# A DLRM tower: tables of 128 rows, ten features looked up by matmul, a ring of row buffers and a new order of steps

## What is computed

```python
e = jnp.stack([tbl_0[ids[:, 0]], ..., tbl_26[ids[:, 26]]], axis=1)      # (512, 27, 128)
z = jnp.einsum('bnd,bmd->bnm', e, e)[:, i, j]                           # i, j = triu_indices(27, k=1): 351 pairs
h = jnp.concatenate([z, dense_ctx], axis=1)                             # (512, 367)
h = jnp.maximum(h @ W_top1 + b_top1, 0.0)                               # 512 wide
h = jnp.maximum(h @ W_top2 + b_top2, 0.0)                               # 256 wide
y = h @ W_top3                                                          # (512, 1)
```

## Time and profile before

| | us |
|---|---|
| median of 3 runs | 169.3 |
| lowest, highest | 168.25, 169.31 |
| profiled execution: span, first to last instruction | 166.6 |
| around the span, by the median | 2.7 |
| PE busy | 119.2 (72%) |
| DVE, ACT busy | 66.6, 65.0 |
| POOL busy (the 72 gathers are 77.2 of it) | 78.1 |

### The profile page before, as it was taken

One profiled execution on the slowest core, in us unless ns is written; L12 is line 12 of the kernel. 1 busy time (PEld: TensorE's weight loads), 2 busy tenths in 40 slices (PEclk: granted clock), 3 DMA queues, 4 the chain that ended last, 5 costly groups with the idle time before them and its releaser, 6 DMA issues.

```text
span 166.6 us, 1949 instructions
## 1 busy us (share of the span) xinstructions
PE 119.2 (72%) x712; PEld 103.3 (62%) x712; DVE 66.6 (40%) x135; ACT 65.0 (39%) x107; POOL 78.1 (47%) x80
## 2 busy tenths in 40 slices
PE   6439949376357095870798997442399999999995
PEld 6437728255245083650677996441299999799993
DVE  3537539372520553770304650200071464346221
ACT  3050948555490553621904650210062263245110
POOL 2377777777777687887800077777200000000000
PEclk9975999999978969699579999655558999999999
DMA  2344444444445466994300036122115003300600
GB/s 47 117 165 145 158 156 159 160 157 156 155 160 162 152 125 161 208 204 148 95 16 4 0 112 142 47 63 51 31 45 115 0 4 102 57 0 29 134 0 4
DMA packets 15751, 16.45 MB, mean 99 GB/s; under 512 B 10099, under 2 KB 12211, under 8 KB 15614
## 3 DMA queue, kind: packets, MB, share of 16 engines
q1 hardware_dynamic: 13308, 11.35, 22.6%
q0 software_dynamic: 2304, 4.72, 11.6%
q10 hardware_dynamic: 130, 0.26, 0.6%
HBM read 14.62 MB, written 1.71 MB: 98 GB/s over the span
## 4 chain that ended last, share of the span: by engine, by line
PE 51%; issue 19%; DMA 12%; another core or an unknown queue 7%; ACT 5%; DVE 4%; SPq 1%; DVEq 0%; ACTq 0%
PE psG L319 18%; PE psG L302 12%; DMA table<-in_tbl 12%; PE psH L333 8%; PE psH L363 5%; PE psT L282 4%; DVE hot L416 3%; PE psG L345 2%; ACT ET L483 1%; PE psH L376 1%; ACT parts L495 1%; ACT hot L502 1%; ACT hot L506 1%; DVE parts L421 1%
## 5 line engine op out<-in xcount | busy, mean ns | idle before, releaser
L269 POOL DMA_INDIRECT rows<-in_tbl,ids_sb x72 | 77.2, 1072 | 38.8 <-issue 21.0
L302 PE MATMUL psG<-hot,parts 125*128 125x512 f32 x156 | 47.7, 470 | 31.3 <-issue 13.9
L302 PEld LDWEIGHTS psG<-hot,parts 125*128 125x128 f32 x156 | 35.8, 235 | 42.1 <-issue 28.5
L319 PE MATMUL psG<-ET 128*122 128x104 f32 x256 | 31.7, 279 | 7.6 <-issue 6.8
L319 PEld LDWEIGHTS psG<-ET 128*122 128x122 f32 x256 | 30.1, 194 | 8.4 <-issue 8.3
L416 DVE TENSOR_SCALAR hot<-pick_ids,row_no 125x512 fp32r<-125x512 int32 x65 | 26.7, 482 | 19.8 <-remote 11.3
L431 DVE COPY gram<-psG 26x208 f32<-26x208 f32 (+1 forms) x17 | 8.2, 485 | 31.9 <-remote 14.5
L523 ACT COPY gram<-psG 26x208 f32<-26x208 f32 (+1 forms) x17 | 8.3, 489 | 31.2 <-PE psG L319 14.3
L421 DVE TENSOR_TENSOR parts<-table,parts 125x1024 fp32r<-125x1024 f32 (+1 forms) x9 | 11.8, 1313 | 20.8 <-ACT parts L495 18.2
L483 ACT COPY ET<-psG 128x512 f32<-128x512 f32 x9 | 9.8, 1085 | 19.1 <-remote 10.4
L495 ACT CAST parts<-table 125x1024 fp32r<-125x1024 f32 (+1 forms) x8 | 9.0, 1128 | 17.5 <-DMA table<-in_tbl 17.5
(11 more groups left out here) (27 smaller groups left out, 45.3 us busy)
## 6 DMA issues: line engine op xcount, KB each, us to landing
table<-in_tbl SPq DMA_DIRECT2D x6, 500.0 KB
pick_ids<-in_picked_ids SPq DMA_DIRECT2D x8, 250.0 KB
table<-in_tbl SPq DMA_DIRECT2D x3, 625.0 KB
pair_blocks<-gram SPq DMA_DIRECT2D x8, 176.0 KB, 1.9
rows<-in_tbl,ids_sb POOLq DMA_INDIRECT x72
w_sb<-in_w SPq DMA_DIRECT2D x1, 1024.0 KB
zT<-pair_blocks SPq DMA_DIRECT2D x12, 60.5 KB
w_sb<-in_w SPq DMA_DIRECT2D x1, 512.0 KB
```

Of the source, the lines that this page charges most:

```text
L269: pool.indirect_dma_start(out=rows[:, t % 2, f, :], out_offset=None, in_=gathered_tables[f], in_offset=bass.IndirectOffsetOnAxis(ap=ids_sb ...
L302: last = pe.matmul(psP[:, k % 2, :], parts[:, k % 2, x, c, :], hot[:, k % 2, c, :], start=x == 0 and c == 0, stop=x == 1 and c == CH[k] - 1)
L319: last = pe.matmul(o, stationary, group[:, :, 1:F], start=True, stop=True)
```

## The change

- V, the partitions of a looked-up table, goes from 125 to 128. The host pads the ten tables with zero rows to 1024 or 1280; a partition still has 8 or 10 rows.
- PICKED goes from 9 to 10: one table of 1250 rows more is looked up, 17 features are gathered (68 indirect DMAs), and a tile's last quad has one feature. BY_ACT changes with it: two chunks only for every other pick with 10 chunks.
- `table` and `pick_ids` have three buffers (TABLES), so SP's waits refer to pick k-3.
- `rows` becomes a ring of 8 quads (RING) over all tiles: the gathers of quad n wait for the transposes of quad n-8.
- The host lays the ids of the gathered features out as one run per partition, and the load (L213) is one plain copy.
- In the loop of the picks the transposes lag by one (LAG), and nine quads, not five, are transposed there.
- `steps` is written anew.

```diff
-    V = 125
+    V = P
-    BY_ACT = [1 if k < NQ else 2 for k in range(FP)]
+    BY_ACT = [1 if CH[k] == min(CH) or k % 2 else 2 for k in range(FP)]
+    TABLES = 3
+    RING = 8
+    LAG = 1
+    DURING_PICKS = FP - LAG
...
-        rows = sb("rows", [P, 2, FG, D])
+        rows = sb("rows", [P, RING, 4, D])
...
-        BY_DVE = [n >= NQ and n % 2 == (NQ + (n // NQ == T - 1)) % 2 for n in range(T * NQ)]
+        BY_DVE = [n >= DURING_PICKS and n % 2 == 0 for n in range(T * NQ)]
...
+        steps = interleaved(units(0), quads(DURING_PICKS, 2 * NQ)) + quads(2 * NQ, 2 * NQ + 2)
+        steps += interleaved(units(1), quads(2 * NQ + 2, 3 * NQ))
+        steps += mlp(0) + quads(3 * NQ, 3 * NQ + 1) + units(2) + [("layer3", 0)]
+        steps += quads(3 * NQ + 1, 3 * NQ + 2) + mlp(1) + quads(3 * NQ + 2, 4 * NQ) + [("layer3", 1)] + units(3)
+        steps += mlp(2) + [("chunk", 0), ("chunk", 1), ("layer3", T - 2), ("chunk", 2), ("chunk", 3),
+                           ("relu1", T - 1), ("layer2", T - 1), ("layer3", T - 1)]
...
-            sp.dma_start(ids_sb[:, :, :], ids.rearrange("(t p) f -> p t f", p=P)).then_inc(ids_in, 16)
+            sp.dma_start(ids_sb[:, :, :], ids).then_inc(ids_in, 16)
             for k in range(FP):
-                if k >= 2:
-                    sp.wait_ge(hot_ready, sum(CH[:k - 1]) - sum(BY_ACT[:k - 1]))
-                    sp.wait_ge(last_hot_ready, sum(BY_ACT[:k - 1]))
+                if k >= TABLES:
+                    sp.wait_ge(hot_ready, sum(CH[:k - TABLES + 1]) - sum(BY_ACT[:k - TABLES + 1]))
+                    sp.wait_ge(last_hot_ready, sum(BY_ACT[:k - TABLES + 1]))
...
-            for t in range(T):
-                if t >= 2:
-                    pool.wait_ge(filled, NQ * (t - 1))
-                for q in range(NQ):
-                    for f in QUADS[q]:
-                        pool.indirect_dma_start(
-                            out=rows[:, t % 2, f, :], out_offset=None, in_=gathered_tables[f],
-                            in_offset=bass.IndirectOffsetOnAxis(ap=ids_sb[:, t, f:f + 1], axis=0),
-                        ).then_inc(gathered[t][q], 16)
+            for n in range(T * NQ):
+                t, q = divmod(n, NQ)
+                if n >= RING:
+                    pool.wait_ge(filled, n - RING + 1)
+                for x, f in enumerate(QUADS[q]):
+                    pool.indirect_dma_start(
+                        out=rows[:, n % RING, x, :], out_offset=None, in_=gathered_tables[f],
+                        in_offset=bass.IndirectOffsetOnAxis(ap=ids_sb[:, t, f:f + 1], axis=0),
+                    ).then_inc(gathered[t][q], 16)
...
-PICKED = 9
+PICKED = 10
```

More of the change, by code:

```diff
@@ L24, in dlrm_tower @@
     P = 128
-    B, FG = ids.shape
-    FP = picked_ids.shape[0]
+    FG = len(gathered_tables)
+    FP, B = picked_ids.shape
     F = FG + FP
@@ L177, in dlrm_tower, with units, quads, interleaved @@
         UNIT_BANKS = [[slice(0, 2)]] * (T * U - 1) + [[slice(0, 1), slice(1, 2)]]
[L182 to L200, removed]
+        def units(t):
+            return [("unit", U * t + u) for u in range(U)]
+        def quads(a, b):
+            return [("quad", n) for n in range(a, b)]
+        def interleaved(many, few):
+            out = []
+            for x, step in enumerate(many):
+                out.append(step)
+                out += few[len(few) * x // len(many):len(few) * (x + 1) // len(many)]
+            return out
+        def mlp(t):
+            return [("layer1", t), ("layer2", t), ("layer2_end", t)]
+        steps = interleaved(units(0), quads(DURING_PICKS, 2 * NQ)) + quads(2 * NQ, 2 * NQ + 2)
[4 more added lines that the diff above has]
+                           ("relu1", T - 1), ("layer2", T - 1), ("layer3", T - 1)]
         block = ctx.enter_context(nc.Block())
@@ L281, in transposes @@
                 for x, f in enumerate(QUADS[q]):
-                    last = pe.transpose(psT[:, n % 2, x, :], rows[:, t % 2, f, :], ident[:, :])
+                    last = pe.transpose(psT[:, n % 2, x, :], rows[:, n % RING, x, :], ident[:, :])
                 last.then_inc(filled, 1)
@@ L381, in _ @@
                 pe.matmul(psH[:, 0, 0, :], ident[:, :], ident[:, :], start=True, stop=True)
-            for x in range(max(FP, NQ)):
-                if x < FP:
-                    pick(x)
-                if x < NQ:
-                    transposes(x)
+            for x in range(FP):
+                pick(x)
+                if x >= LAG:
+                    transposes(x - LAG)
             pe.wait_ge(pad_zero, T)
@@ L614 @@
         "in_dense": np.ascontiguousarray(np.asarray(inputs["dense_ctx"]).T),
-        "in_ids": np.ascontiguousarray(ids[:, gather]),
+        "in_ids": np.ascontiguousarray(ids[:, gather].reshape(-1, 128, len(gather)).transpose(1, 0, 2)),
         "in_picked_ids": np.ascontiguousarray(ids[:, pick].T),
@@ L623 @@
     for f in gather + pick:
-        arrays[f"in_tbl_{f}"] = np.ascontiguousarray(inputs[f"tbl_{f}"])
+        table = np.asarray(inputs[f"tbl_{f}"])
+        if f in pick:
+            table = np.concatenate([table, np.zeros((-len(table) % 128, table.shape[1]), table.dtype)])
+        arrays[f"in_tbl_{f}"] = np.ascontiguousarray(table)
     nc = bacc.Bacc("TRN2", target_bir_lowering=False, num_devices=1)
```

31 lines of the change are left out of this document (15 added, 16 removed).

## The result

Timed together, the changed kernel took 164.25 us (median of 4 runs, 161.46 to 169.3) and the kernel before 169.31 (4 runs, 168.25 to 174.06). The ratio is 0.959, with an interval of 0.952 to 0.967: 4% faster. The ratio compares the fast runs of each (161.46 and 161.97 for the changed kernel); the medians of all four give 0.970. The prediction had 129 us and a range of 121 to 149. It was wrong by 35 us, and the time lies outside its range.

A forecast was written before the change was run, and what follows sets the result against it. Loads bound the picks, and a stall followed at 103 to 120 us. Forecast: gathers end at 95, last quad 97.5, tail 22.8, clock 2, late signals 4: span 126.3, plus 2.7 gives 129 us; range 121 to 149.

The forecast's parts named there:

- I take 4 net: Addition to the span for PE's signals arriving late at handovers while gathers run: 4 us.
- The rival: PE's signals stay late while gathers run, from tile 0's units on: span 142 to 146, time 147 us; chance 0.27.
- the reads of short rows: Tile 0's short-row reads, now at about 66 us, meet gathers until 97; the late-signal stretch was to begin there.
- The clock's term: PE waiting between quads at clock 0.85 over 37 us of work: 5.5 us more, eating the spare 5; 2 us taken.
- the ring's part: With 8 quads in the ring PE stays ahead after the picks, POOL never stops and its 12.0 us wait goes.
- 38x1.38: 38 gathers beside the picks at 1.38 us each, part of a 91.4 us sum for POOL's 68 gathers.
- picks 4.9 and 5.1: Pick loop: 4.9 us for each small pick and 5.1 for each large one, so picks are over at 55 us.
- the rule that says so: A two-port VectorE operation shuts GpSimd out of its port; denser compares would bring gathers nearer the dear end, 105 us.
- 128 rows spread the loads: Table loads use 16 engines instead of 5; two loads' 11.2 us become about 3.5. Rival that they don't: 152 us, chance 0.12.
- Three buffers at nothing: A third table buffer lets loads start a pick earlier; valued at nothing while loads are fast.
- The ring removes the 12 us wait: Quad n waits for quad n-8, so POOL's 12.0 us wait before tile 3's gathers goes.
- The tenth pick takes four gathers away: Looking up one more table costs a pick of 5.1 us and removes 4 gathers.

The follow-up runs named there:

- p1: The kernel before with 128-row tables alone (two table buffers, nine picks, halves, old order): 131.99 us, ratio 0.904 to the kernel before.
- t1: The changed kernel with all of DVE's compares written as tensor_tensor instead of tensor_scalar: 131.53 us, ratio 0.906 to the kernel before.

## Why the prediction was wrong

Two steps failed, of different size.

*"I take 4 net" for late signals* is the large one. On a chip of the first kind they cost the changed kernel 28 to 31 us (161.5 to 164.25 against 133.61) and before 23 (169.31 against 145.92). I had seen the stall, given its cause as unknown, and still gave the case in which it goes the greater chance. The rival had the sign, the place (from tile 0's units on) and the gathers as the partner right, at 147; the reads of short rows it had wrong. It was too low because I set its pace by unit 7's 0.7 us per pair; in fact nothing was signalled from 75.1 to 99.5, and again for 7 us before 117.6. Its sum was short as well: of twelve units three are done at its pace, and it adds one and tile 2's four; with tile 1's four at 1.75 us each it gives 154, still 10 too low. (The clock's term is slightly off too: 37 us of work at 0.85 take 6.5 more, not 5.5; I took 2.) It may also have had the ring's part wrong. In before, POOL paused at 55.8 and at 83.4, where the rows' halves made it wait; in the changed kernel it issued 59 gathers until 95.5. If long holds end with pauses, a change that removes POOL's waits makes them longer. That is argued from the table above and not shown: on such a chip the ring was never tried alone.

*"38x1.38" for the gathers beside picks and "picks 4.9 and 5.1"* is the smaller one, and the only one on a chip of the second kind, 133.6 against 129. By its own terms there:

| step | forecast | chip of the second kind |
|---|---|---|
| ids, first gather | 3.7 | 5.57 |
| picks over | 55 | 64.5 |
| gathers over | 95 | 106.0 |
| last quad transposed | 97.5 | 109.2 |
| from there to the end | 22.8 | 22.4 |
| clock and signals | 6 | not seen apart |
| span | 126.3 | 131.6 |

The 9.5 us by which the picks end late are their waits for rows (9.7); their own pace was below the forecast, 4.0 and not 4.9 for a small one, as LAG = 3 shows. The tail and the sum over PE's work held. The ids came hardly sooner than before. The gathers cost 80.0 + 67 x 0.30 = 100 us where I had 91.4, most of the difference beside the picks: 1.36 + 0.30 = 1.66 each in 8:42, not 1.38. I named the rule that says so, weighed it as one that moves the sum towards its dear end (all at 1.49, over at 105), took 95 all the same, and did not see that before's 1.077 was a mean over sparse compares (65 in 77 us) and that the change packs them. A price that depends on overlap must be taken per overlap. Split that way the trace of before already had 0.94 (the median of 50 gathers) beside no compare and 1.24 (the mean of the 18 that run beside compares for over 0.4 us); the changed kernel has 0.94 and 1.69. And the slower gathers then hold the picks, through one-pick-late transposes: the two terms that I summed apart are one.

*128 rows spread the loads*: right. The queue's share of the 16 engines in 10:50 goes from 28.4% to 53.4% (the changed kernel on the second kind of chip; 28.4% with 125 rows again), and the Trainium skill's rule on the number of engines ("DMA: Bandwidth & Descriptors", "Why a DMA increments its semaphore by 16 and not by 1") agrees with that, with 131.99 against 145.92 for that edit alone, and with 7.0 us per pick again when it is undone. *Three buffers at nothing*: not contradicted (130.48 and 135.08 with two, 133.61 with three). *The ring removes the 12 us wait*: on the second kind of chip, where before's is 8.6, the changed kernel has none, but so do 128 rows alone (p1's 72 gathers run from 5.6 to 105.3 with no wait), and the ring alone gives a ratio of 1.000. *The tenth pick takes four gathers away*: yes, but with nine picks the 72 gathers end at 107.8, so it saves 1.8 us and not the 5 of four gathers, and p1's 72 end at 105.3. The rest of the change together gains nothing on top of the 128 rows (133.61 against 131.99).

## What to carry to other kernels

Make the outermost dimension of a load one that 16 divides before anything else is tuned: here, where the signals were on time, that one constant gave 14 of 146 us and the rest nothing. When a faster engine runs beside gathers that GpSimd issues, price the gathers by what DVE does during each of them, and treat both as one resource; packing tensor_scalar compares closer can make the kernel slower, as LAG = 3 did. And time a change on more than one chip before its mechanism is argued: the same pair differed by 4% on one and by 8% on another.

## What the hardware showed that was not expected

- Chips (or times) of two kinds. Before took 145.1, 145.9, 146.4 and 145.4 us in four groups and 169.3 and 170.5 in two, with nothing between. In the latter two PE's completions reach the other engines up to 28 us late while POOL issues gathers, and the longest holds end 3 to 5 us after it pauses.
- An indirect DMA costs POOL 0.94 + 0.30 us with 128 rows and 0.91 + 0.30 with 64, and up to 5.06 us where DVE does not pause between tensor_scalar compares and subtractions (the changed kernel timed beside t1; 4.66 with LAG = 3).
- Compares of ids as tensor_tensor leave gathers alone, though both inputs are in SBUF; the subtraction, a tensor_tensor too, can add 0.49 (1.43 at 15.44, while it runs from 14.83). In before and in t1 a gather that starts while a subtraction runs takes about 0.8 us plus what is left of the subtraction (1.43 with 0.61 left, 1.82 with 1.00 left; one of t1, begun together with it, took 0.94), and one that is under way when the subtraction starts takes 0.94 to 0.95. What tells the two apart wasn't tried; one input of the compare is one word repeated.
